# An attention and feed-forward block on one core: normalising and residual by GpSimd, and rows of the first batch through memory

## What is computed

```python
x = x + _layernorm(attn(_layernorm(x)))        # x: 8 batches x 256 tokens x 128
x = x + _layernorm(ffn(_layernorm(x)))

# attn: 16 heads of 8, with a bias that depends on i - j
qkv = x @ W_qkv + b_qkv
scores = einsum('bihd,bjhd->bhij', q, k) / sqrt(8) + rel_bias[clip(i - j + 128, 0, 256)]
out = einsum('bhij,bjhd->bihd', softmax(scores), v) @ W_out + b_out

# ffn: ternary weights 512 x 128 and 512 x 512, each output with a scale
h = silu(x @ w1.T * s1) * (x @ w2.T * s2)
h = gelu(h @ h1.T * h1s)
h = gelu(h @ h2.T * h2s)
y = h @ w3.T * s3
```

## Time and profile before

| | us |
|---|---|
| three runs | 292.56, 290.83, 291.42 (median 291.42) |
| the profiled execution | 292.18 |
| its span, first to last instruction | 290.4 |
| busy in it: PE, DVE, ACT, POOL | 268.5, 219.3, 205.9, 102.4 |
| mean granted PE clock | 0.991 of full |

### The profile page before, as it was taken

One profiled execution on the slowest core, in us unless ns is written; L12 is line 12 of the kernel. 1 busy time (PEld: TensorE's weight loads), 2 busy tenths in 40 slices (PEclk: granted clock), 3 DMA queues, 4 the chain that ended last, 5 costly groups with the idle time before them and its releaser, 6 DMA issues.

```text
span 290.4 us, 5171 instructions
## 1 busy us (share of the span) xinstructions
PE 268.5 (92%) x1875; PEld 180.4 (62%) x1875; DVE 219.3 (76%) x442; ACT 205.9 (71%) x316; POOL 102.4 (35%) x107
## 2 busy tenths in 40 slices
PE   7999989899999999999998998899999999999980
PEld 7756645555555554565554554567887888888860
DVE  3489977889789889889889899848556843673674
ACT  2777777776786786885886876777469976896750
POOL 7616000103504305906966957018630202400111
PEclk9999999999999999999999999999999999999996
DMA  6979506232221263470320200000000000010012
GB/s 166 320 238 142 184 11 208 89 83 77 74 76 38 77 207 124 138 224 8 104 81 19 61 1 3 1 3 1 0 2 0 0 0 2 0 36 2 2 36 77
DMA packets 21356, 21.17 MB, mean 73 GB/s; under 512 B 3664, under 2 KB 18768, under 8 KB 21072
## 3 DMA queue, kind: packets, MB, share of 16 engines
q1 hardware_dynamic: 20464, 20.53, 24.8%
q10 hardware_dynamic: 864, 0.27, 0.4%
HBM read 14.90 MB, written 5.64 MB: 71 GB/s over the span
## 4 chain that ended last, share of the span: by engine, by line
PE 60%; DVE 22%; ACT 9%; issue 5%; DMA 1%; POOL 0%; SPq 0%; ACTq 0%; DVEq 0%
PE place L1441 10%; PE place L1442 10%; PE place L1244 8%; DVE mx L685 7%; PE pv L1296 6%; PE place L1236 4%; ACT ring L1008 4%; DVE y_and_z L620 4%; PE place L1270 4%; DVE stats L609 2%; PE place L1195 2%; DVE place L692 2%; ACT place L1015 2%; PE pv L1442 2%; PE pv L1441 2%
## 5 line engine op out<-in xcount | busy, mean ns | idle before, releaser
L685 DVE TENSOR_REDUCE mx<-place 128x4 f32<-128x1024 f32 x64 | 78.1, 1222 | 13.1 <-PE place L1244 11.8
L517 POOL TENSOR_TENSOR rstd<-mv,mhalf 128x2 f32<-128x2 f32 (+1 forms) x26 | 21.0, 809 | 153.0 <-DVE mv L617 153.0
L1008 ACT ACTIVATE ring<-place 128x1024 f32<-128x1024 f32 x64 | 65.6, 1027 | 6.3 <-PE place L1281 3.0
L1244 PE MATMUL place<-room,identr 128*128 128x512 f32 x128 | 46.9, 447 | 0.0
L1015 ACT COPY place<-raw 128x1024 f32<-128x1024 f32 x37 | 37.7, 1022 | 12.2 <-DVE mx L685 11.9
L1441 PE MATMUL place<-room,w_hi 128*128 128x512 f32 (+1 forms) x116 | 44.6, 387 | 0.7 <-DVE room L818 0.7
L1442 PE MATMUL place<-room,w_hi 128*128 128x512 f32 (+1 forms) x116 | 44.0, 382 | 0.0
L818 DVE TENSOR_TENSOR room<-ring,room 128x512 fp32r<-128x512 f32 x32 | 21.4, 690 | 18.5 <-ACT room L1096 18.5
L1296 PE MATMUL pv<-ring,vx 128*9 128x256 f32 x512 | 33.6, 380 | 0.0
L1270 PE MATMUL place<-room 33*128 33x256 f32 x256 | 31.7, 328 | 1.1 <-DVE place L692 1.0
L1236 PE MATMUL place<-room 33*128 33x256 f32 x256 | 28.3, 297 | 2.9 <-ACT ring L1008 2.7
(11 more groups left out here) (141 smaller groups left out, 442.9 us busy)
## 6 DMA issues: line engine op xcount, KB each, us to landing
raw<-ext SPq DMA_DIRECT2D x8, 384.0 KB, 6.9
room<-q_parts SPq DMA_DIRECT2D x48, 64.0 KB
room<-k_parts SPq DMA_DIRECT2D x48, 64.0 KB
w_lo<-h SPq DMA_DIRECT2D x2, 1024.0 KB, 5.2
q_parts<-w_hi SPq DMA_DIRECT2D x4, 256.0 KB, 3.0
k_parts<-w_hi SPq DMA_DIRECT2D x2, 512.0 KB, 3.4
xs<-x SPq DMA_DIRECT2D x3, 256.0 KB, 5.7
w_lo<-w SPq DMA_DIRECT2D x3, 256.0 KB, 2.7
```

What stands on the lines that cost most here:

```text
L517: nc.gpsimd.tensor_tensor(rstd[:, at:at + width], mv[:, at:at + width, 1], mhalf[:, 0:width], ALU.pow).then_inc(rstd_set, 1)
L685: nc.vector.tensor_reduce(mx[:, s // RPAIRS, :, :, s % RPAIRS].rearrange("p i k -> p k i"), max_tile(b * PAIRS + s)[:, :, :].rearrange("p ...
L1008: nc.scalar.activation(probs[:, s % PRING, :, :, :].rearrange("p k j n -> p (k j n)"), score_tile(b * PAIRS + s)[:, :, :].rearrange("p k n ...
L1244: last = mm(max_tile(b * PAIRS + s)[:, half, :], identr[:, :], windows(table_hi[:, 2 * s + half, :], 0, P, 2, S), start=False, stop=True, ...
```

## The change

Three things are changed, and their semaphore counts with them.

1. Batch 0 makes only the rows of pairs 0 to 3 directly (`RPAIRS` is 4). For pairs 4 to 7 unit 0 gets q and k (banks 2 and 3), which are stored like those of the other units and loaded as rows; PE waits for `first_rows_in` ahead of pair 4. The constant rows that SP writes once now cover pairs 4 to 7 of the first buffer as well. The tiles for `take` move to another place of SBUF.
2. `x_normalize` of units 2 to 4, `residual` and `second_norm` go from DVE to POOL. DVE keeps the moments: `x1_moments` stands at s = 6, behind maxima(b + 1, 6). POOL casts table pieces 0 and 1 ahead of its third power. DVE takes the moments of unit 1 later.
3. In the feed-forward order, `project(B - 1)` stands behind three outputs of layer 1 of chunk 1, where there were two.

```diff
@@ -183,7 +183,7 @@
 
-        TBANK, QBANK, KBANK, VBANK = (7, 7, 6, 7, 7), (None, 5, 6, 7, 7), (None, 4, 7, 7, 7), (6, 6, 6, 7, 7)
+        TBANK, QBANK, KBANK, VBANK = (7, 7, 6, 7, 7), (2, 5, 6, 7, 7), (3, 4, 7, 7, 7), (6, 6, 6, 7, 7)
...
@@ -364,7 +365,7 @@
 
             if i == 0:
-                eng.wait_ge(rows_set, 2 * PAIRS)
+                eng.wait_ge(rows_set, 2 * RPAIRS)
...
@@ -411,7 +412,9 @@
                 to = 64 * half + KROWS
                 for rows, src in ((q_rows, zeros), (k_rows, ones)):
-                    sp.dma_start(rows[to:to + 1, 1, :, :].bitcast(F32), src[0:PAIRS, :].bitcast(F32)).then_inc(extra_in, 16)
+                    flat = rows[to:to + 1, :, :, :].rearrange("p a s n -> p (a s) n")
+                    sp.dma_start(flat[:, RPAIRS:2 * PAIRS, :].bitcast(F32),
+                                 src[0:2 * PAIRS - RPAIRS, :].bitcast(F32)).then_inc(extra_in, 16)
...
@@ -431,13 +434,13 @@
                 for i, dram in enumerate((q_dram, k_dram)):
-                    sp.wait_ge(qk_hi_set, (u - 1) * 2 + i + 1)
+                    sp.wait_ge(qk_hi_set, u * 2 + i + 1)
                     hi = qk_hi[u][:, i, :].bitcast(F32)
                     if i == 0:
                         sp.dma_start(dram[0, :, tok], hi).then_inc(parts_out[u], 16)
                     else:
...
@@ -463,7 +466,10 @@
 
+            store_parts(0)
             store_parts(1)
+            sp.wait_ge(parts_out[0], PARTS_OUT)
+            row_dmas(0, RPAIRS, RPAIRS, first_rows_in)
             sp.wait_ge(parts_out[1], PARTS_OUT)
             row_dmas(1, 0, PAIRS, second_rows_in)
             load_x(4)
...
@@ -525,16 +531,54 @@
+            def normalize(dst, src, t, at=0):
+                return nc.gpsimd.tensor_scalar(dst, src, mv[:, at + t, 0:1], rstd[:, at + t:at + t + 1],
+                                               ALU.subtract, ALU.mult)
+
+            def x_normalize(u):
+                first, tiles = UNITS[u]
+                pool.wait_ge(rstd_set, u + 1)
+                if u >= 3:
+                    pool.wait_ge(xnT_ready, 2 if u == 3 else 4)
+                for t in range(tiles):
+                    last = normalize(x_norm[u][:, t, :], xs[:, first + t, :], t, first)
+                last.then_inc(xn_set, 1)
+
+            def residual(b):
+                inv_std(b * 2 + NU + 1, TPB)
+                pool.wait_ge(rstd_set, b * 2 + NU + 1)
+                for t in range(TPB):
+                    last = normalize(y[:, t, :], y[:, t, :], t)
+                last.then_inc(y_norm, 1)
+                pool.wait_ge(y_norm, b + 1)
+                xb = xs[:, TPB * b:TPB * b + TPB, :]
+                nc.gpsimd.tensor_tensor(xb, xb, y[:, :, :], ALU.add).then_inc(x1_set, 1)
+
+            def second_norm(b):
+                inv_std(b * 2 + NU + 2, TPB)
+                pool.wait_ge(rstd_set, b * 2 + NU + 2)
+                if b > 0:
+                    pool.wait_ge(zT_ready, b)
+                for t in range(TPB):
+                    last = normalize(z[:, t, :], xs[:, b * TPB + t, :], t)
+                last.then_inc(z_set, 1)
+
             x_inv_std(0)
             pool.wait_ge(qk_w_in[1], 16)
             pool.wait_ge(row_zeros, 1)
             spread_weights(nc.gpsimd.tensor_copy, 1)
             x_inv_std(1)
+            table_high(0)
+            table_high(1)
             x_inv_std(2)
-            for s in range(PAIRS):
+            table_high(2)
+            x_normalize(2)
+            for s in range(3, 6):
                 table_high(s)
-                if s == 5:
-                    x_inv_std(3)
+            x_inv_std(3)
+            x_normalize(3)
+            table_high(6)
+            table_high(7)
             for i, s in enumerate(BY_PE):
                 pool.wait_ge(table_hi_pool, s + 1)
...
@@ -542,6 +586,7 @@
             x_inv_std(4)
+            x_normalize(4)
...
@@ -573,8 +618,8 @@
             for b in range(B):
                 if b > 0:
-                    inv_std((b - 1) * 2 + NU + 1, TPB)
-                    inv_std((b - 1) * 2 + NU + 2, TPB)
+                    residual(b - 1)
+                    second_norm(b - 1)
...
@@ -658,11 +701,11 @@
             x_moments(0)
             dve.wait_ge(qk_w_in[0], 16)
             nc.vector.tensor_scalar(wq_sb[:, :], wq_sb[:, :], scale, None, ALU.mult).then_inc(bq_scaled, 1)
-            x_moments(1)
             x_normalize(0)
             dve.wait_ge(row_zeros, 1)
             dve.wait_ge(bq_scaled, 1)
             spread_weights(nc.vector.tensor_copy, 0, (0,))
+            x_moments(1)
             dve.wait_ge(brows_in, 16)
             nc.vector.tensor_scalar(brows_sb[:, 0, 0:PAIRS], brows_sb[:, 0, 0:PAIRS], scale, None,
                                     ALU.mult).then_inc(brows_scaled, 1)
...
@@ -670,12 +713,14 @@
                                     ALU.mult).then_inc(low_bias_set, 1)
-            x_normalize(1)
             dve.wait_ge(ident_loaded, 16)
             nc.vector.tensor_scalar(minus_ident[:, :], ident[:, :], -1.0, None, ALU.mult).then_inc(minus_set, 1)
+            x_normalize(1)
             dve.wait_ge(qk_w_in[2], 16)
             nc.vector.tensor_scalar(bq_sb[:, 0:1], bq_sb[:, 0:1], scale, None, ALU.mult).then_inc(bq_scaled, 1)
             nc.vector.tensor_copy(identr[:, :], ident[:, :]).then_inc(identr_set, 1)
+            q_and_k_low(0, 0)
+            q_and_k_low(0, 1)
...
@@ -714,27 +759,15 @@
                                         ALU.add).then_inc(y_read, 1)
                 dve.wait_ge(y_read, b + 1)
+                if b > 0:
+
+                    dve.wait_ge(z_set, b)
                 moments(lambda t: y[:, t, :], TPB, b * 6 + base + 2)
 
-            def residual(b):
-
-                dve.wait_ge(rstd_set, b * 2 + NU + 1)
-                for t in range(TPB):
-                    last = normalize(y[:, t, :], y[:, t, :], t)
-                last.then_inc(y_norm, 1)
-                dve.wait_ge(y_norm, b + 1)
-                xb = xs[:, TPB * b:TPB * b + TPB, :]
-                nc.vector.tensor_tensor(xb, xb, y[:, :, :], ALU.add).then_inc(x1_set, 1)
+            def x1_moments(b):
+
                 dve.wait_ge(x1_set, b + 1)
                 moments(lambda t: xs[:, b * TPB + t, :], TPB, b * 6 + base + 4)
-
-            def second_norm(b):
-                dve.wait_ge(rstd_set, b * 2 + NU + 2)
-                if b > 0:
-                    dve.wait_ge(zT_ready, b)
-                for t in range(TPB):
-                    last = normalize(z[:, t, :], xs[:, b * TPB + t, :], t)
-                last.then_inc(z_set, 1)
 
...
@@ -787,8 +817,6 @@
                         if s == 6:
                             x_moments(4)
-                        if s == 7:
-                            x_normalize(4)
...
@@ -798,10 +826,8 @@
-                        if s == 5:
-                            residual(b - 1)
                         if s == 6:
-                            second_norm(b - 1)
+                            x1_moments(b - 1)
                             if b in (2, 3):
                                 q_and_k_low(4, b - 2)
                             if b == 4:
...
@@ -975,16 +1000,17 @@
             take(0)
             keep_xT(1)
+            act.wait_ge(bq_scaled, 2)
+            q_and_k_high(0, 0)
+            q_and_k_high(0, 1)
             take(1)
             keep_rows(0)
-            act.wait_ge(bq_scaled, 2)
             q_and_k_high(1, 0)
...
@@ -993,12 +1019,8 @@
             keep_xT(2)
-            take(PAIRS - 2)
+            q_and_k_high(2, 0)
             minus_max(0, 0)
-            keep_rows(PAIRS - 2)
-            take(PAIRS - 1)
-            q_and_k_high(2, 0)
-            keep_rows(PAIRS - 1)
...
@@ -1205,6 +1227,9 @@
             x_T(1)
+            pe.wait_ge(bq_scaled, 1)
+            q_and_k(0, 0)
+            q_and_k(0, 1)
             pe.wait_ge(minus_set, 1)
...
@@ -1329,13 +1354,19 @@
             pe.wait_ge(identr_set, 1)
             for s in range(PAIRS):
-                if s + 1 < PAIRS:
+                if s + 1 < RPAIRS:
                     row_lows(s + 1)
-                if s + 2 < PAIRS:
+                if s + 2 < RPAIRS:
                     row_products(s + 2)
+                if s == 0:
+
+                    pe.wait_ge(qk_lo_set, 2)
+                if s == RPAIRS:
+                    pe.wait_ge(first_rows_in, SECOND_DMAS * 16)
+                    pe.wait_ge(extra_in, 4 * 16)
                 if s == 1:
 
-                    pe.wait_ge(qk_lo_set, 2)
+                    pe.wait_ge(qk_lo_set, 4)
...
@@ -1560,9 +1591,9 @@
                 layer1(0, 3, exact)
-                whole(layer1, 1, exact, (0, 1))
+                whole(layer1, 1, exact, (0, 1, 2))
                 project(B - 1)
-                whole(layer1, 1, exact, (2, 3))
+                whole(layer1, 1, exact, (3,))
                 whole(layer2, 0, exact)
```

37 lines of the change are left out of this document (16 added, 21 removed).

## The result

The changed kernel takes 309.63 us in the median of four runs (306.94 to 312.78); the kernel before takes 291.64 beside it. The ratio is 1.0585 (95% interval 1.0492 to 1.0678), so the change costs 18.0 us by the medians. The forecast was 292.6, in a range of 290.0 to 295.0. The profiled execution took 306.94 us with a span of 304.9, which is 14.5 us more span than before.

A forecast was written before the change was run, and what follows sets the result against it. The prediction took PE to bound the kernel, with relief for DVE worth little by itself. Its terms, +0.9 + 0.5 + 0 + 0.5 - 0.7 = +1.2 us on 291.42, gave 292.6 us, range 290.0 to 295.0.

The forecast's parts named there:

- What bounds the kernel: Whole kernel: PE is the bound, busy 268.5 of 290.4 us; relief for DVE pays only where PE waits for it.
- Part 1, the rows: First batch, pairs 4 to 7: rows there at 25.2, PE waits 4.3 us; +0.9 us, plus +0.5 for the clock.
- The loop's start at 33.8 plus 0.5 for the clock: First scores of the loop, held to 33.8 by SP's queue (32.98 before), 0.5 us more for PE's lower clock.
- (b): Rival, slower: the wait at pair 4 lowers PE's clock and delays the loop; head +3.5 us, 294.7 us, chance 0.18.
- The bound of +2.0: Head of the kernel: upper bound of the loss if unit 1's stores delay unit 0's by a microsecond; value taken +0.9.
- Part 2: Head: x normalising of units 2 to 4 on GpSimd, two table pieces ahead; 0 us, bounds -0.2 and +0.5.
- Part 3, the size of the wait: Loop, z's transposition: at 0.5 us per GpSimd normalising PE waits about 0.76 us; +0.5 us over all batches.
- Part 3, the last two batches: Last two batches with z: PE's waits, up to 1.05 us before, become 0.76; gains of 0.3 and 0.2 us.
- Part 3, the clock: Loop, behind PE's waits for z: the sum has no term for a lower clock; it was priced only at pair 4.
- Part 4: Feed-forward: the last batch's projection moved back loses its 0.69 us wait; -0.7 us, bounds -0.7 and 0.
- (c): Rival, slower: a GpSimd normalising costs 0.7 us, each z 0.8 late, DVE waits for splitting; 294.6 us, chance 0.17.
- The sum: Whole kernel: +0.9 + 0.5 + 0 + 0.5 - 0.7 = +1.2 us, median 292.6 us.

The follow-up runs named there:

- all_but_norms: The changed kernel with the residual and second norm back on DVE in their old places; 295.77 us, ratio 1.0143 to the kernel before.
- blanks_z: The changed kernel with twelve blank matmuls on PE ahead of its wait for z in six batches; 302.67 us, ratio 1.0370 to the kernel before.
- pool_probe: The kernel before with eleven more GpSimd instructions late in the feed-forward part, on an unused buffer, to time them; 291.15 us in one run.
- x1_first: The kernel before with residual and second norm on GpSimd, moments of x1 ahead of the maxima of pair 6; 299.28 us, ratio 1.0221.

## Why the prediction was wrong, step by step

- **What bounds the kernel** (PE, and relief for DVE is worth little): right. DVE is busy 21 us less in the changed kernel, and nothing is gained by it.
- **Part 1, the rows.** PE at pair 4 at 20.9: it was there at 21.75. x_T(1) was to lose half of what x_T(0) gained by the new order; it lost more, and came at 9.75 where it had come at 9.15:

```profile
9.75 0.44 PE L1191 MATMUL misc<-ident,xn 128*128 128x128 f32 x2 [0.81 <-DVE xn L665]
```

  Rows at 25.2: 25.37 in the profiled run, which is partly luck, since they came 1 to 2 us later in the other five. The loop's start at 33.8 plus 0.5 for the clock: 35.23, and 36.4 to 37.2 in the other kernels with the trip. The queue on SP (the first rows, batch 1's rows, mrow) was a real limit, but rival (b)'s condition is what held: PE's rest at the lower clock, 9.86 us (9.5 in the forecast), was longer than the queue's, about 9.1 (8.6). The bound of +2.0 and (b)'s +3.5 were nearer than the value taken. The 0.21 us a blank that the forecast read as the lower level come from a stretch where the trace's granted clock reads 1.00; the ratio of two that it took is borne out by the rows here (1.91 us for 1.02, at 0.50). What the forecast did not have at all is the second batch: its mrow comes late too, by 1.12 us here and by 1.36 in all_but_norms, where the clock falls behind it. By the runs this part costs about 5 us against +1.4.
- **Part 2** at 0: right, slightly to the good (ratio 0.9984).
- **Part 3, the size of the wait.** The sum for z held term by term, with the price on GpSimd mis-sized: 0.78 us instead of 0.5, and some 0.15 more of signals and gaps around the power. That makes 1.51 us of wait instead of 0.76. The batch up to 121.72 grew by 0.89 us where 0.27 was forecast. The price lay outside the 0.3 to 0.7 of the range, because a row of another operation was scaled by its columns, and the form with two operations was not priced apart.
- **Part 3, the last two batches** were to gain 0.5 us. They have the longest waits, 1.97 and 2.34 us, in which the residual on GpSimd (1.58 + 0.73 us) makes x1 late by 0.36 and 0.73 us for DVE.
- **Part 3, the clock.** This is the step that failed most: the term for the lower clock in the loop, which the sum left at nothing without a reason. The forecast priced the lower clock at pair 4 and left it out of the loop, although by its own sum PE would pause for some 0.75 us in each batch there. By blanks_z the lower clock behind them costs 7.0 us by the medians. The Trainium skill (TensorE: Matmul & The Clock Gate, Why this matters for your kernels) warns of gaps between bursts of matmuls, but of longer ones than any wait in this loop; by it these six would be harmless. The trace of the changed kernel doesn't bear that out for three of them (1.51, 1.52 and 2.34 us), behind which the granted clock fell to 0.50; behind the other three it held.
- **Part 4** at -0.7: right on the kernel before (-0.6). In the changed kernel the gain is lost, since PE waits for GpSimd's last z, which the forecast had 1.9 us ahead of PE. GpSimd's and PE's rows:

```profile
244.57 3.29 POOL L535 TENSOR_SCALAR y_and_z<-xs,mv,rstd 128x128 f32<-128x128 f32 x2
```

```profile
248.01 0.41 PE L1352 MATMUL misc<-ident,y_and_z 128*128 128x128 f32 x2 [1.42 <-POOL y_and_z L535]
```

  The two instructions take 3.29 us there, 1.64 each, twice their price in the loop. DVE works beside them, but in pool_probe it did too, at 0.78 each; the cause is open.
- **The rivals.** (c), GpSimd's instruction at 0.7, had the right place and sign and half of the mechanism, the waits; at 0.78 and with the clock behind it, which (c) did not have, it is 13.4 us instead of the 2.5 that it gave. (b) had the clock, but only at pair 4.
- **The sum**, by medians and by difference: about 5 us for the head (+1.4 forecast), 6.4 for the waits in the loop (+0.5), 7.0 for the clock in the loop (not in the sum), -1.0 for parts 2 and 4 (-0.7). That is 17.4 of the 18.0 measured, against +1.2.

## What to carry to other kernels

A pause of an engine that is otherwise always busy has two prices: its length, and what the clock does behind it. Where a change puts a new wait of one or two microseconds into a dense stream of matmuls, reckon with the clock falling behind it, and fill it with blank matmuls before judging the change. Price an instruction on GpSimd by a row with the same number of operations and the same number of elements, not by scaling another. And before moving work from DVE to GpSimd to make it quicker, see whether DVE is slow only because GpSimd works beside it.

## What the runs showed of the hardware

- On GpSimd, subtract-and-multiply takes about 0.8 us for 128x128 (1.64 once, at the last z) whether the two numbers are constants or scalars per partition, and 1.54 for 128x256 with scalars; with one operation it is 0.61, a copy 0.54. DVE takes 0.30 for the same, or 0.85 while GpSimd splits weights.
- PE's granted clock can fall to 0.50 behind a wait of 1.1 us (x1_first) to 2.3 us (the changed kernel) and then stays there for 3 to 10 us; it does not behind every such wait, and twelve blank matmuls in the wait kept it at 1.00 in all six batches.
- Eight row loads of 64 KB that were all issued by 23.3 or 23.4 us on two queues reached their reader at 26.5 and 27.6.
